# Adding the bias of two feed-forwards on VectorE instead of on TensorE

## The chip, the cores and the metric

The kernel runs on one core of a Trainium2 chip. The metric is the device time of one execution, in microseconds (us); lower is better. A core has TensorE (PE, matrix products into PSUM; PEld is its loading of weights), VectorE (DVE), ScalarE (ACT), GpSimd (POOL) and SyncE (SP), whose queue issues transfers. They run side by side and wait for each other at semaphores.

## The reference

The input is 4096 rows of 256 numbers. Six layers follow each other, each added to its input after a layer norm: a gated feed-forward, a gated delta-rule attention, the feed-forward again, then a binary feed-forward, a state space layer and the binary feed-forward again with the same weights. The change touches the two binary ones:

```
def _L1_ffn_ref(x, weights, scale, bias):
    w = (weights >= 0.0).astype(x.dtype) * 2.0 - 1.0
    y = jnp.einsum('bsi,oi->bso', x, w)
    y = y * scale + bias
    y = jnp.clip(y, -MAX_VAL, MAX_VAL)      # 100
    return y
...
x = x + 0.5 * _L1_ffn_ref(_layernorm(x), weights, scale, bias)
```

## The kernel before, in words

The program has seven phases, one after the other; each engine has its own sequence of instructions, and between two phases all engines wait for each other (L172). The phases of interest are the last three: `binary` pass 0 (from 988 us), `space` (the state space layer, from 1051 us) and `binary` pass 1 (from about 1186 us, its products from 1197 us).

The rows are held as 32 tiles of 128 rows. A *block* is four tiles (8 blocks), a *pair* is two tiles (16 pairs, P0 to P15, two per block). For a pass:

- ScalarE normalizes the rows of a block (L518) with factors that GpSimd works out from VectorE's statistics. In pass 1, VectorE makes the statistics (L312, L313) of block b+3 just before it takes out the pairs of block b, GpSimd makes its factors (L304 to L307; L306 is a power) just before it adds the pairs of block b, and ScalarE normalizes block b+3 when it has copied the turned block b+1.
- TensorE turns a block (L625, eight records) and ScalarE copies it from PSUM (L670). TensorE's order is: products of block b, turning of block b+2.
- For each pair, TensorE fills one bank of PSUM (128 x 512): first a product that writes the bias into both halves (L636: a 64x128 matrix of 1/32 with a 64x256 matrix of the bias, its first 32 rows being the rounded half bias and the next 32 what the rounding left), then four products with `w_bin` on top (L641, eight records in the trace). Pair p uses bank p mod 4 and waits until pair p-4 has been taken out.
- VectorE takes the pair out of PSUM with a clip to -50 and 50 (L710) into `Y`; GpSimd adds `Y` to the rows (L747).

The factor 0.5 is folded into weights and bias beforehand: at the start of pass 0, VectorE multiplies `w_bin` by half the scale (L700), halves the bias row (L701) and makes the two parts for the product (L696, L702, L703); TensorE's first product waits for `b_weights`, raised by the last of these.

Pass 0 has more in it, for the layer behind it. SP moves each finished block into another order of rows (L764, eight transfers per block). VectorE makes statistics of the moved block b-2 after the pairs of block b, GpSimd its factors (L555 to L558, block b-3), ScalarE its rows from b = 4 on. From block 5 on TensorE also flips two stretches of rows (L576), VectorE multiplies them by gamma (L581, before the pairs) and GpSimd adds beta (L587, after the pairs). In pass 1 SP sends each finished block out (L769).

`own.seq` makes an engine wait for its own instruction before the next one. `bcast_mid(row, 2)` reads a row of 256 twice, for the two halves of a bank.

Of the kernel before, what the change touches and what calls it, by code (L numbers as in the profile page):

```python
# [6 lines left out]
F32R = mybir.dt.float32r  # L7
I32 = mybir.dt.int32
ALU = mybir.AluOpType
# [3 lines left out]
P = 128  # L13
DM = 256
KD = DM // P
# [38 lines left out]
def bcast_mid(ap, n):  # L54
    return ap.unsqueeze(1).to_broadcast([ap.shape[0], n, ap.shape[1]])
# [14 lines left out]
def build(nc, io):  # L70
    ctx = ExitStack()
    with ctx:
# [6 lines left out]
        B = Box()  # L79
# [41 lines left out]
        S = Box()  # L121
# [12 lines left out]
        made = {}  # L134

        def phase_memory(kind, shape, within=None):

            mem = ExitStack()

            def take(name, cols):  # L140
                return mem.enter_context(nc.sbuf_tensor(f"{kind}_{name}", [P, cols], F32))[:]

            M = Box()
            if within is not None:
                within(M)
            shape(M, take)
            made[kind] = M
            return mem

        phase_memory("ffn", ffn_memory).close()  # L150
        both = phase_memory("both", shared_memory)
# [7 lines left out]
        phase_memory("delta", delta_memory, of_both).close()  # L159
        both.close()  # L160
        late = phase_memory("late", late_memory)
        B.X2, B.MV2, B.rows = made["late"].X2, made["late"].MV2, made["late"].rows
        B.rstd2, B.shift2, B.U, B.N2 = made["late"].rstd2, made["late"].shift2, made["late"].U, made["late"].N2
        B.bias_parts, B.thirty_second = made["late"].bias_parts, made["late"].thirty_second
        phase_memory("binary", binary_memory).close()
        phase_memory("space", space_memory).close()
        late.close()
# [142 lines left out]
def tile_stats(v, own, B, X, MV, t):  # L310
    s = B.stats[:, 6 * (t % BLK):6 * (t % BLK) + 6]
    own.seq(v.bn_stats(s, X[:, t, :]))  # L312
    return v.bn_aggr(MV[:, t, :], s)  # L313
# [229 lines left out]
def moved_stats(v, own, B, S, b):  # L543

    v.wait_ge(S.late_in[b], 64 + 128)
    for t in (2 * b, 2 * b + 1, TB + 2 * b, TB + 2 * b + 1):
        i = tile_stats(v, own, B, B.X2, B.MV2, t)
    i.then_inc(S.m_stats, 1)
# [22 lines left out]
def input_flip(pe, B, S, k):  # L571

    pe.wait_ge(S.n_xn, k + 1)
    if k >= 2:
        pe.wait_ge(S.n_gamma, k - 1)
    pe.matmul(B.bank[6 + k % 2][:], B.flip, B.N2[k % 2], start=True, stop=True).then_inc(S.n_flip, 1)  # L576


def input_strength(v, B, S, k):
    v.wait_ge(S.n_flip, k + 1)  # L580
    v.tensor_tensor(both_of(B.U, k), two(B.bank[6 + k % 2][:]), bcast_mid(B.rows[2], 2), ALU.mult).then_inc(S.n_gamma, 1)  # L581
# [17 lines left out]
def late_memory(M, take):  # L599

    M.X2 = take("X", NT * DM).rearrange("p (t d) -> p t d", t=NT)
    M.MV2 = take("mean_var", 2 * NT).rearrange("p (t two) -> p t two", two=2)
    M.rstd2, M.shift2 = take("rstd", NT), take("shift", NT)
    M.U = take("U", NT * DM).rearrange("p (t d) -> p t d", t=NT)
    M.N2 = [take(f"N2{i}", 2 * DM) for i in range(2)]
    M.rows = [take(f"{n}_row", DM) for n in ("scale", "bias", "gamma", "beta")]
    M.bias_parts, M.thirty_second = take("bias_parts", DM), take("thirty_second", P)


def binary_memory(M, take):  # L610
# [5 lines left out]
def binary_tensor(pe, B, M, S, run):  # L616
    blocks, pairs = run * NBLK, run * NT // 2

    def turn(b):
        pe.wait_ge(S.b_xn, blocks + b + 1)  # L620
        for k in range(KD):
            if blocks + b > 0:
                pe.wait_ge(S.b_xt, 2 * (blocks + b - 1) + k + 1)
            for j in range(BLK):
                i = pe.transpose(B.bank[4 + k][:, j * P:(j + 1) * P], M.xn[b % 2][:, j * DM + k * P:j * DM + (k + 1) * P], B.ident)  # L625
            i.then_inc(S.b_xt_ps, 1)

    def project(b):
        pe.wait_ge(S.b_xt, 2 * (blocks + b) + 2)
        pe.wait_ge(S.b_weights, 1)  # L630
        for h in range(2):
            p = 2 * b + h
            if p >= 4:
                pe.wait_ge(S.b_clip, pairs + p - 3)
            o = B.bank[p % 4]
            pe.matmul(o.rearrange("p (j n) -> p j n", j=2), B.thirty_second[0:64, :].bitcast(F32R),  # L636
                      B.bias_parts[0:64, :].bitcast(F32R).unsqueeze(1).to_broadcast([64, 2, DM]),
                      start=True, stop=False, skip_group_check=True)
            for j in range(2):
                for k in range(KD):  # L640
                    i = pe.matmul(o[:, j * DM:(j + 1) * DM], M.XT[b % 3][k][:, (2 * h + j) * P:(2 * h + j + 1) * P],  # L641
                                  B.w_bin[:, k * DM:(k + 1) * DM], start=False, stop=(k == KD - 1), skip_group_check=True)
            i.then_inc(S.b_mm, 1)

    turn(0)
    turn(1)
    for b in range(NBLK):
        if run == 0 and b >= FLIP_LAG:
            input_flip(pe, B, S, 2 * (b - FLIP_LAG))
            input_flip(pe, B, S, 2 * (b - FLIP_LAG) + 1)  # L650
        project(b)
        if b + 2 < NBLK:
            turn(b + 2)
# [30 lines left out]
def binary_vector(v, own, B, M, S, run):  # L684
    pairs = run * NT // 2

    def stats(b):
        for t in range(BLK * b, BLK * b + BLK):
            i = tile_stats(v, own, B, B.X2, B.MV2, t)
        i.then_inc(S.b_stats, 1)  # L690

    def weights():

        scale_row, bias_row = B.rows[0], B.rows[1]
        parts = B.bias_parts.bitcast(F32R)
        v.tensor_scalar(B.thirty_second[0:64, :].bitcast(F32R), B.ident[0:64, :], 0.0, 1.0 / 32, ALU.mult, ALU.add)  # L696
        v.wait_ge(S.rows_in, 64)
        for k in range(KD):
            w = B.w_bin[:, k * DM:(k + 1) * DM]
            v.scalar_tensor_tensor(out=w, in0=w, scalar=0.5, in1=scale_row, op0=ALU.mult, op1=ALU.mult)  # L700
        own.seq(v.tensor_scalar(bias_row, bias_row, 0.5, None, ALU.mult))  # L701
        own.seq(v.tensor_copy(parts[0:64, :], bias_row[0:64, :]))  # L702
        v.tensor_tensor(parts[32:64, :], bias_row[32:64, :], B.bias_parts[32:64, :], ALU.subtract).then_inc(S.b_weights, 1)  # L703

    def clip(b):
        for p in (2 * b, 2 * b + 1):
            v.wait_ge(S.b_mm, pairs + p + 1)
            if p >= 4:
                v.wait_ge(S.b_x, pairs + p - 3)
            v.tensor_scalar(M.Y[p % 4], B.bank[p % 4], -50.0, 50.0, ALU.max, ALU.min).then_inc(S.b_clip, 1)  # L710

    if run == 0:
        weights()
    else:
        for b in range(3):
            stats(b)
    for b in range(NBLK):
        if run == 1 and b + 3 < NBLK:
            stats(b + 3)
        if run == 0 and b >= FLIP_LAG:  # L720
            input_strength(v, B, S, 2 * (b - FLIP_LAG))
            input_strength(v, B, S, 2 * (b - FLIP_LAG) + 1)
        clip(b)
        if run == 0 and b >= STATS_LAG:
            moved_stats(v, own, B, S, b - STATS_LAG)
# [1460 lines left out]
```

## Time and profile before

| | |
|---|---|
| Three timed runs | 1249.26, 1244.98, 1247.41 us; median 1247.41 |
| Profiled execution | 1248.46 us; its span, first to last instruction, 1246.7 us |
| Mean granted TensorE clock | 0.92 |
| Busy: PE, PEld | 1041.7 us (84%), 743.2 us (60%) |
| Busy: DVE, ACT, POOL | 935.5 us (75%), 601.0 us (48%), 520.3 us (42%) |
| L641, the products of the pairs | 256 records, 66.8 us busy |
| L710, the clip from PSUM | 32 instructions, 22.1 us busy |

A time in the trace is counted from the start of the span. An instruction's row gives its start, its duration, its engine and line, what it writes and reads, and in brackets how long its engine had been idle and who released it. TensorE's records overlap and their ends are modelled, so that the distance between two starts says more than a duration. The granted clock is 1.0 at TensorE's upper level and 0.5 at its lower; a mean between the two is a window in which it changed.

### The profile page before, as it was taken

Reading aid. Unit: us, or ns where it says so; the run is one execution under the profiler, and the core shown is the slowest. Engines: PE = TensorE matmul, PEld = TensorE weight load, DVE = VectorE, ACT = ScalarE, POOL = GpSimd, SP = SyncE. Lnnn points to the kernel's source line nnn. Section 1 sums busy time; section 2 is a strip of 40 time slices with the busy share of each in tenths; the row PEclk is TensorE's granted clock in tenths of the full one; section 3 lists DMA queues with packets and bytes.
Section 4 is the critical chain, followed back from the end, with each engine's and each line's share of the span. In section 5 each row is a group of like instructions: output and inputs, shape, how many; then the busy total and the mean of one; then the engine's idle time right before and its main releaser. Section 6 shows DMA issues by size and latency. Waiting matters only on the chain. (4 is left out here: it accounts for less than half of the span.)

```text
span 1246.7 us, 38552 instructions
## 1 busy us (share of the span) xinstructions
PE 1041.7 (84%) x15542; PEld 743.2 (60%) x15542; DVE 935.5 (75%) x2403; ACT 601.0 (48%) x1614; POOL 520.3 (42%) x772
## 2 busy tenths in 40 slices
PE   2999977777888888888898876579999798799878
PEld 2888853444555555555565655458888674355456
DVE  3777736378899999999999988527776445899853
ACT  2433345435666767677766664554333343101052
POOL 2666530423444334444344443216666257400055
PEclk9999988887899999999999987769999798899979
DMA  9000013344344434344434432100000023954013
GB/s 249 20 2 1 1 56 110 79 97 105 82 97 103 96 91 102 80 106 103 97 91 92 100 90 70 37 3 1 1 1 1 18 66 95 244 153 118 1 34 101
DMA packets 220160, 93.30 MB, mean 75 GB/s; under 512 B 143440, under 2 KB 209872, under 8 KB 219984
## 3 DMA queue, kind: packets, MB, share of 16 engines
q1 hardware_dynamic: 212240, 79.83, 26.1%
q0 software_dynamic: 6144, 8.40, 2.8%
q10 hardware_dynamic: 1600, 2.62, 0.7%
q8 instruction: 123, 2.02, 0.7%
q14 instruction: 53, 0.43, 0.1%
HBM read 56.20 MB, written 30.41 MB: 69 GB/s over the span
## 5 line engine op out<-in xcount | busy, mean ns | idle before, releaser
L1762 DVE TENSOR_TENSOR delta_tmp<-delta_PR 128x130 f32<-128x130 f32 (+12 forms) x416 | 162.3, 390 | 9.4
L1759 DVE TENSOR_TENSOR delta_PR<-delta_PR,delta_tmp 128x130 f32<-128x130 f32 (+12 forms) x416 | 157.7, 379 | 9.4
L1886 POOL TENSOR_TENSOR delta_S<-delta_E,delta_Bm 128x128 f32<-128x128 f32 x32 | 15.2, 476 | 226.7 <-issue 220.1
L1414 PE MATMUL psum<-delta_T,delta_pad 128*32 128x128 f32 x2048 | 82.3, 328 | 30.7 <-DMA delta_T<-inverse_scratch 29.8
L1613 ACT ACTIVATE delta_y<-psum 32x128 f32<-32x128 f32 x256 | 68.7, 268 | 59.8 <-PE psum L1448 56.9
L1414 PEld LDWEIGHTS psum<-delta_T,delta_pad 128*32 128x32 f32 x2048 | 70.2, 134 | 41.5 <-DMA delta_T<-inverse_scratch 34.8
L507 POOL TENSOR_TENSOR ffn_H<-ffn_hid,ffn_H 128x512 fp32r<-128x512 f32 x48 | 61.6, 1289 | 59.2 <-DVE ffn_H L473 59.2
L507 POOL TENSOR_TENSOR first_H<-first_hid,first_H 128x512 fp32r<-128x512 f32 x48 | 61.6, 1289 | 53.0 <-DVE first_H L473 53.0
L1629 ACT ACTIVATE delta_wide<-delta_S 32x128 f32<-32x128 f32 x256 | 78.2, 305 | 3.2
L1398 PE MATMUL psum<-delta_MV,delta_KT 32*32 32x128 f32 x2048 | 69.6, 289 | 10.7 <-ACT delta_E L1563 10.7
L1873 POOL DMA_DIRECT2D delta_Kd<-key_scratch x128 | 74.7, 590 | 0.1
L1398 PEld LDWEIGHTS psum<-delta_MV,delta_KT 32*32 32x32 f32 x2048 | 59.4, 113 | 22.4 <-ACT delta_E L1563 15.5
L1358 PE MATMUL psum<-both_w_in,delta_xT 128*128 128x512 f32 x128 | 66.7, 645 | 3.3 <-DVEq L172 2.1
L439 ACT ACTIVATE first_silu<-psum 128x512 f32<-128x512 f32 x48 | 28.8, 599 | 83.3 <-PE psum L392 83.3
L439 ACT ACTIVATE ffn_silu<-psum 128x512 f32<-128x512 f32 x48 | 28.8, 599 | 81.1 <-PE psum L392 81.1
L312 DVE BATCH_NORM_STATS2 ln_stats<-X 128x6 f32<-128x256 f32 x128 | 54.1, 423 | 17.4 <-DMA X<-in_x 14.8
L641 PE MATMUL psum<-w_bin,binary_XT 128*128 128x256 f32 x256 | 66.8, 406 | 0.0
L1368 PE MATMUL psum<-both_w_in,delta_xT 128*128 128x512 f32 x128 | 64.4, 627 | 0.0
L710 DVE TENSOR_SCALAR binary_Y<-psum 128x512 f32<-128x512 f32 x32 | 22.1, 692 | 54.0 <-PE psum L641 53.9
L1850 POOL TENSOR_TENSOR delta_VK<-delta_QK,both_eg 128x256 f32<-128x256 f32 x32 | 21.1, 660 | 88.7 <-DVE delta_QK L1694 88.5
L1461 PEld LDWEIGHTS psum<-delta_y,delta_Kd 32*32 32x32 f32 x2048 | 23.1, 111 | 57.5 <-ACT delta_y L1613 57.5
L392 PE MATMUL psum<-first_XT,w_gate 128*128 128x512 f32 x192 | 54.0, 404 | 3.7 <-DVE first_XT L461 3.7
(284 smaller groups left out, 2685.6 us busy)
## 6 DMA issues: line engine op xcount, KB each, us to landing
within_scratch<-delta_PT SPq DMA_DIRECT2D x128, 64.0 KB, 1.9
delta_PR<-within_scratch SPq DMA_DIRECT2D x16, 512.0 KB, 4.4
inverse_scratch<-delta_PR SPq DMA_DIRECT2D x16, 512.0 KB, 3.0
space_T<-taps_scratch SPq DMA_DIRECT2D x8, 1024.0 KB, 5.9
X<-taps_scratch SPq DMA_DIRECT2D x8, 1024.0 KB, 8.8
X<-in_x SPq DMA_DIRECT2D x32, 128.0 KB, 9.9
turned_scratch<-gates_XT SPq DMA_DIRECT2D x16, 256.0 KB, 2.3
delta_xT<-turned_scratch SPq DMA_DIRECT2D x32, 128.0 KB, 3.0
```

Source lines behind the costliest of these rows:

```text
L439: a.activation(M.silu[n % 3], B.bank[n % 2][:], ACT.Silu, scale=1.0 / 127.0).then_inc(S.silu, 1)
L507: g.tensor_tensor(lo.bitcast(F32R), M.hid[n % 3], hi, ALU.subtract).then_inc(S.hid_lo, 1)
L641: i = pe.matmul(o[:, j * DM:(j + 1) * DM], M.XT[b % 3][k][:, (2 * h + j) * P:(2 * h + j + 1) * P], B.w_bin[:, k * DM:(k + 1) * DM], start= ...
L1358: i = pe.matmul(bank[4][:], M.xT[t % 2][:, k * P:(k + 1) * P], M.w_in[:, k, 0:512], start=(k == 0), stop=(k == 1))
L1368: i = pe.matmul(bank[5][:], M.xT[t % 2][:, k * P:(k + 1) * P], M.w_in[:, k, 512:1024], start=(k == 0), stop=(k == 1))
L1398: mm = pe.matmul(kk[g][rows, q * P:(q + 1) * P], M.KT[rows, g * P + SUB * q:g * P + SUB * q + SUB], M.MV[rows, (4 * g + q) * P:(4 * g + q ...
L1414: i = pe.matmul(bank[3][SUB * c:SUB * c + SUB, (2 * w + g) * P:(2 * w + g + 1) * P], M.pad[:, from_c:from_c + SUB], M.T[t % 2][:, h * P:(h ...
L1613: i = a.activation(dst, heads(bank[6][rows, half * P:(half + 1) * P]), ACT.Copy)
L1629: i = a.activation(states(M.wide[half])[rows, :, SUB * c:SUB * c + SUB], states(X)[rows, :, :], ACT.Copy)
L1759: i = v.tensor_tensor(after, after, t3, ALU.add)
L1762: i = v.tensor_tensor(t3, column.to_broadcast([P, j, n_after]), row.to_broadcast([P, j, n_after]), ALU.mult)
L1873: g.dma_start(dst, src).then_inc(S.k_in[t % 2], 16)
```

## The change

The product of the bias goes, and with it its two matrices. A pair's four products start the bank themselves. VectorE adds the halved bias row as it takes the pair out of PSUM, into `Y`, waits for that, and clips `Y` in place in SBUF. `b_weights` is raised by the second product of weights and scale; the halving of the bias row stands behind it.

```diff
 def late_memory(M, take):
-    M.bias_parts, M.thirty_second = take("bias_parts", DM), take("thirty_second", P)
...
 def project(b):
...
             o = B.bank[p % 4]
-            pe.matmul(o.rearrange("p (j n) -> p j n", j=2), B.thirty_second[0:64, :].bitcast(F32R),
-                      B.bias_parts[0:64, :].bitcast(F32R).unsqueeze(1).to_broadcast([64, 2, DM]),
-                      start=True, stop=False, skip_group_check=True)
             for j in range(2):
                 for k in range(KD):
                     i = pe.matmul(o[:, j * DM:(j + 1) * DM], M.XT[b % 3][k][:, (2 * h + j) * P:(2 * h + j + 1) * P],
-                                  B.w_bin[:, k * DM:(k + 1) * DM], start=False, stop=(k == KD - 1), skip_group_check=True)
+                                  B.w_bin[:, k * DM:(k + 1) * DM], start=(k == 0), stop=(k == KD - 1))
             i.then_inc(S.b_mm, 1)
...
 def weights():
         scale_row, bias_row = B.rows[0], B.rows[1]
-        parts = B.bias_parts.bitcast(F32R)
-        v.tensor_scalar(B.thirty_second[0:64, :].bitcast(F32R), B.ident[0:64, :], 0.0, 1.0 / 32, ALU.mult, ALU.add)
         v.wait_ge(S.rows_in, 64)
         for k in range(KD):
             w = B.w_bin[:, k * DM:(k + 1) * DM]
-            v.scalar_tensor_tensor(out=w, in0=w, scalar=0.5, in1=scale_row, op0=ALU.mult, op1=ALU.mult)
+            i = v.scalar_tensor_tensor(out=w, in0=w, scalar=0.5, in1=scale_row, op0=ALU.mult, op1=ALU.mult)
+        i.then_inc(S.b_weights, 1)
         own.seq(v.tensor_scalar(bias_row, bias_row, 0.5, None, ALU.mult))
-        own.seq(v.tensor_copy(parts[0:64, :], bias_row[0:64, :]))
-        v.tensor_tensor(parts[32:64, :], bias_row[32:64, :], B.bias_parts[32:64, :], ALU.subtract).then_inc(S.b_weights, 1)
...
 def clip(b):
         for p in (2 * b, 2 * b + 1):
             v.wait_ge(S.b_mm, pairs + p + 1)
             if p >= 4:
                 v.wait_ge(S.b_x, pairs + p - 3)
-            v.tensor_scalar(M.Y[p % 4], B.bank[p % 4], -50.0, 50.0, ALU.max, ALU.min).then_inc(S.b_clip, 1)
+            y = M.Y[p % 4]
+            both = B.bank[p % 4].rearrange("p (j n) -> p j n", j=2)
+            own.seq(v.tensor_tensor(y.rearrange("p (j n) -> p j n", j=2), both, bcast_mid(B.rows[1], 2), ALU.add))
+            v.tensor_scalar(y, y, -50.0, 50.0, ALU.max, ALU.min).then_inc(S.b_clip, 1)
```

## Rows read from the trace of the kernel before

**Rows 1.** The chain that ended last, in order of time: start us, us, what.
```profile
1197.14 0.72 PE psum L636
...
1200.65 0.43 PE psum L636
1201.08 1.92 PE psum L641 x8
1203.00 0.87 PE psum L625 x8
```

**Rows 2.** Window of pass 1: busy us of PE, PEld, DVE, ACT, POOL; clock; DMA.
```profile
1197.00:1242.20 45.20, 44.19 (x193) 32.29 (x192) 19.05 (x48) 17.75 (x36) 25.85 (x32) 0.97 0.24 82
```

**Rows 3.** Single lines of VectorE: duration ns min/median/max, first and last start.
```profile
L710 DVE TENSOR_SCALAR binary_Y<-psum x32: 691/692/693, 1000.1 to 1241.2; 128x512 f32<-128x512 f32 x32
...
L581 DVE TENSOR_TENSOR late_U<-psum,late_gamma_row x16: 656/682/692, 1028.2 to 1090.6; 128x512 f32<-128x512 f32 x16
...
L478 DVE TENSOR_SCALAR first_raw_bin<-first_raw_bin x1: 421/421/421, 130.4 to 130.4; 128x512 f32<-128x512 f32 x1
```

**Rows 4.** Timeline around the start of pass 0: start us, us, engine.
```profile
994.44 0.28 DVE L701 TENSOR_SCALAR late_bias_row<-late_bias_row 128x256 f32<-128x256 f32 x1
994.76 0.28 DVE L702 CAST late_bias_parts<-late_bias_row 64x256 fp32r<-64x256 f32 x1
995.08 0.41 DVE L703 TENSOR_TENSOR late_bias_parts<-late_bias_row,late_bias_parts 32x256 fp32r<-32x256 f32 x1
...
995.64 0.76 PE L636 MATMUL psum<-late_bias_parts,late_thirty_second 64*128 64x512 f32 x1 [3.18 <-DVE late_bias_parts L703]
...
996.33 3.78 PE L641 MATMUL psum<-w_bin,binary_XT 128*128 128x256 f32 x8
...
1000.76 2.38 PE L641 MATMUL psum<-w_bin,binary_XT 128*128 128x256 f32 x8
```

**Rows 5.** Windows of 1 us, columns as in rows 2: the clock is 0.70 and 0.72.
```profile
1001.00:1002.00 1.00, 1.00 (x4) 0.86 (x5) 0.00 (x0) 0.00 (x0) 1.00 (x1) 0.70 0.00 0
...
1199.00:1200.00 1.00, 1.00 (x5) 0.84 (x4) 0.00 (x0) 1.00 (x3) 0.00 (x0) 0.72 0.00 0
```

**Rows 6.** Timeline of GpSimd in pass 0, from block 5.
```profile
1028.41 0.24 POOL L555 TENSOR_SCALAR late_shift<-late_mean_var 128x4 f32<-128x4 f32 x1 [0.88 <-DVE late_mean_var L313]
...
1037.38 0.24 POOL L555 TENSOR_SCALAR late_shift<-late_mean_var 128x4 f32<-128x4 f32 x1
...
1040.85 1.27 POOL L747 TENSOR_TENSOR X<-binary_Y,X 128x512 f32<-128x512 f32 x1 [0.32 <-DVE binary_Y L710]
...
1044.67 0.24 POOL L555 TENSOR_SCALAR late_shift<-late_mean_var 128x4 f32<-128x4 f32 x1
...
1049.00 2.48 POOL L587 TENSOR_TENSOR late_U<-late_U,late_beta_row 128x512 f32<-128x512 f32 x2
```

**Rows 7.** Timeline of one block in pass 1: statistics, factors, rows.
```profile
1203.65 0.42 DVE L312 BATCH_NORM_STATS2 ln_stats<-late_X 128x6 f32<-128x256 f32 x1
...
1205.95 0.24 POOL L304 TENSOR_SCALAR ln_shift<-late_mean_var 128x4 f32<-128x4 f32 x1 [0.87 <-DVE late_mean_var L313]
...
1207.91 2.08 ACT L518 ACTIVATE binary_xn<-late_X,ln_shift,ln_rstd 128x256 f32<-128x256 f32 x4 [3.35 <-POOL ln_shift L307]
```

**Rows 8.** Timelines where a CAST of VectorE meets GpSimd.
```profile
945.05 1.29 POOL L507 TENSOR_TENSOR ffn_H<-ffn_hid,ffn_H 128x512 fp32r<-128x512 f32 x1
945.10 1.52 DVE L473 CAST ffn_H<-ffn_hid 128x512 fp32r<-128x512 f32 x1
...
131.41 1.04 POOL L306 TENSOR_TENSOR ln_rstd<-ln_rstd,minus_half 128x4 f32<-128x4 f32 x1
131.88 0.43 DVE L473 CAST first_H<-first_hid 128x512 fp32r<-128x512 f32 x1
```

**Rows 9.** Timeline of SP's queue: the last block moved in pass 0.
```profile
1049.07 5.06 SPq L764 DMA_DIRECT2D late_X<-X  x8
```

**Rows 10.** Timeline of GpSimd: the last addition of pass 1.
```profile
1242.00 1.26 POOL L747 TENSOR_TENSOR late_X<-binary_Y,late_X 128x512 f32<-128x512 f32 x1 [1.09 <-DVE binary_Y L710]
```

More of the change, by code:

```diff
@@ L163, in build @@
         B.rstd2, B.shift2, B.U, B.N2 = made["late"].rstd2, made["late"].shift2, made["late"].U, made["late"].N2
-        B.bias_parts, B.thirty_second = made["late"].bias_parts, made["late"].thirty_second
         phase_memory("binary", binary_memory).close()
```

## The prediction

> **What bounds the kernel now.** I read the page's chain first, then the stages around the change, then single instructions. The binary feed-forward is computed twice: pass 0 begins near 988 us, pass 1 near 1197 us; I call their 16 bank-sized products P0 to P15. The chain in order of time [rows 1] shows pass 1 as TensorE from end to end: a bias product (0.43 us, the first 0.72 at the lower clock), four 128x256 products in 1.92, and after every second pair the turning of a block, 0.87. The stage table agrees: TensorE is busy for 44 of 45 us, VectorE for 19, GpSimd for 26 [rows 2]. What ends pass 0 is GpSimd instead: its last two offset additions run to 1051.48, and from its factors at 1037.38 on it has no idle except 0.32 us [rows 6].
>
> **The change part by part.** *The weights.* TensorE now waits for the second weight product instead of for L703. Those three bias instructions stand between 994.44 and 995.49; TensorE started at 995.64, 0.15 after [rows 4]. It will start near 994.6, 1.0 earlier. The constant of 1/32 that goes was made under the wait for the rows: nothing.
>
> *The bias products.* 32 go, 0.43 us each at the upper clock and 0.72 at the lower [rows 1]. All sit on TensorE's own sequence.
>
> *The addition.* VectorE's one instruction from PSUM (0.69) becomes an addition from PSUM and a row, then a clip in SBUF. The first is the shape of L581 (PSUM and a row repeated, 128x512): 0.68. The second is the shape of L478 (SBUF to SBUF, 128x512): 0.42 [rows 3]. The wait on its own semaphore between them is about 0.03, the gap between L701 and L702 (994.76 after 994.44 + 0.28 [rows 4]). So 1.14 in place of 0.69: +0.45 per pair, 14.4 us more VectorE work in 32 pairs. The bank is released 0.45 later too, but a product waits for the release of the fourth before it, over 7 us back: no cost.
>
> Is VectorE then the bound? In pass 1 its block is four statistics (from 1203.65 to just before GpSimd takes them up at 1205.95: 2.2) and two pairs (2.3): 4.5 us. TensorE's block goes from 5.57 to 2 x 1.92 + 0.87 = 4.71. GpSimd's is its factors (1205.95 to 1207.88, when ScalarE takes them up: 1.93) and two additions of 1.26: 4.5 [rows 7, 10]. All three fit, with 0.2 us to spare. TensorE stays the bound if nobody holds VectorE up.
>
> *The lock.* Something does. At 945.10 a CAST of 128x512 in SBUF, alone 0.43, lasts 1.52 beside a GpSimd addition that had begun 0.05 before: it ended 0.28 after it. But at 131.88 a CAST of that shape runs in its full 0.43 inside GpSimd's small power operation [rows 8]. I take it that the new clip is held for up to 1.1 by GpSimd's 128x512 additions, and not by its small factors; the addition from PSUM isn't held. The Trainium skill, page "SBUF — State Buffer", section "Who interferes with whom", states this lock for a whole instruction, with any GpSimd instruction; the first row agrees with it and the second doesn't.
>
> *Pass 1, walked.* The clock rises at 1199.56 (mean 0.72 over 1199 to 1200 [rows 5]), whoever is running. Four products are eight records: 3.78 / 8 = 0.47 us each at the lower clock [rows 4], 1.92 / 8 = 0.24 at the upper [rows 1]. P0 now starts them at 1197.14: 2.42 us at the lower clock are 5.1 records, the other 2.9 take 0.69, and it ends at 1200.25, 0.4 earlier than 1200.65. Then 15 x 1.92 and six turnings of 0.87 put P15 at 1234.3, where by the same count (15 x 2.35) it was 1241.1; GpSimd's last addition began at 1242.00, 0.09 + 0.69 behind 1241.2 [rows 10]. VectorE: pairs P0 and P1 are clipped by 1203.35, statistics of block 4 end at 1205.5, its factors at 1207.5; P2 is clipped at 1206.6, but its addition must wait for the factors and takes GpSimd at 1207.5, just as the clip of P3 wants it at 1207.6: held to 1209.0. Statistics of block 5 end at 1211.2. Walked on in the same way, blocks 6 and 7 follow at 1215.7 and 1220.2, with no hold or one more. Block 7's factors are there at 1222.6 and its rows (four, 2.07) at 1224.7; its turning comes at 1225.7. No turning waits, by a margin of 1 us. The tail grows by the +0.45 behind P15. Gain: 6.9 - 0.45 = 6.4 us.
>
> *Pass 0, walked.* The 1.0 from the weights; P0 and P1 mostly run before the clock rises (at about 1001.7; if that moves with the start, at 1000.6), so P1 ends at 1001.3 to 1001.9 in place of 1003.14 [rows 4, 5]: I take 1.55. Eight pairs of 0.43 more make 5.0 at the end of P9: 1020.5, where 1003.14 + 8 x 2.35 + 4 x 0.87 was 1025.4. A part is given back by the lag of VectorE and GpSimd: the clip of P7 meets the addition of P6 and is held to 1017.8, statistics of block 1 end at 1020.0, their factors at 1022.0, only then come the additions of P8 and P9, to 1024.9. So GpSimd's block 5 begins near 1024.95, 3.45 earlier than 1028.41. From there GpSimd is the bound: its block is 7.29 (1037.38 to 1044.67) less 0.32 = 6.97, the last 6.81, so 20.75 in three blocks, where they took 23.07 [rows 6]: 2.3 more. VectorE's clips hold it up in turn (0.42 at most, some two times): -0.7. TensorE (flips 1.7, pairs 3.84, turning 0.87: 6.4) and VectorE (two strengths 1.25, pairs 2.3, statistics 2.2, holds 1 to 1.5: 7.0) are below or beside it. Transfers of a moved block take SP 5.06 [rows 9] and pass 0's early blocks now come every 4.7, so SP lags, but by my walk each block lands 1 to 4 us before its statistics. Gain: 3.45 + 2.3 - 0.7 = 5.0 us, with bounds 2.5 (each of six clips holds GpSimd up and is held) and 6.8 (no lock).
>
> *The stage between* starts cold on TensorE in both kernels, after 5 us of idleness now and 8 then, so it moves as a whole: nothing.
>
> **Sum.** 5.0 + 6.4 = 11.4 us. The profiled execution took 1248.46 (span 1246.7 and 1.8 around it), 1.05 above the median of the three timed runs; against the median, 1247.41 - 11.4 = 1236.0. 0.3% (3.7 us) is about what a measurement of this kernel can tell from no change.
>
> **The rivals.**
> 1. *The lock makes VectorE the pace of pass 1.* If GpSimd's power operation (1.04) holds the clip as well, the first clip of a block waits 0.9 and the second 0.9 to 1.1: VectorE's block becomes 6.0, for the four blocks with statistics. Block 7's statistics end at 1223.5, its turning at 1228.5, P15 at 1236.2: 1.9 lost; pass 0 loses about as much. Total gain 7 to 8: 1239.5. The row at 131.88 speaks against, the margin of 0.2 us per block for. 25%. It is the result that the skill's rule for whole instructions (the same page and section) would give.
> 2. *Pass 0 gives nothing.* GpSimd, VectorE and SP together keep the old pace there, and only pass 1 and the start gain: 6.4 to 7.5, so 1240.5. For: GpSimd ends the pass, and no work leaves it [rows 6]. Against: it has 2.3 us to catch up from block 5 on, and before that it followed TensorE's pace of 5.57 with a block of 4.5. 10%.
> 3. *The gain vanishes in new waits,* less than 3.7 us left: every clip held for 1.09 (VectorE's block 6.7) and every addition of GpSimd held for 0.42: P15 near 1242 and pass 0 gains 2.5. 1245. 6%.
> 4. *Slower: TensorE loses its clock.* It stands at the lower level after the 3.2 us of idleness before 995.64, for some 6 us [rows 4, 5]. If statistics, factors and rows of a block (2.2 + 1.9 + 2.1) came late enough to idle TensorE by 3 us before each of four turnings, each would cost 3 and some 2.5 to 3 at half speed: 4 x 5.8 = 23 against 11.4, so 1259. It decides from the second such gap on (2 x 5.8 = 11.6). My margin at the turnings is 1 us, and a lag of VectorE of 0.2 to 1 us per block doesn't make gaps of 3. 5%.
> The forecast itself, gains of 9 to 12.8: 54%, its own range 1234.5 to 1238.5.
>
> **How the numbers follow.** The likeliest case gives 1236.0. The range reaches down to no lock and a full 6.8 in pass 0 (13.3: 1234) and up past rivals 1 and 2 to 1242; 85% of the chance lies in it. Faster by over 0.3%: the forecast, rivals 1 and 2 = 0.89. Within 0.3%: 0.06. Slower: 0.05.
>
> **What would show it.** In the profile after: no L636; pass 1's chain on TensorE as 1.92, 1.92, 0.87 with no gap above 0.2; the new addition at 0.68 and the clip at 0.42 when free, 1.0 to 1.5 in about one of four; GpSimd without idle from block 5 of pass 0 and its end near 1046.5; pass 1's P15 35 to 38 us after the start of P0, against 44.0. Wrong would be: clips held inside the power operation, turnings waiting for ACT's rows, a phase end of pass 0 later than 1049, or a clock below 1.0 after the first 4 us of either pass.

## The result, and the profile after

The kernel after takes 1231.16 us (median of five timed runs, 1228.71 to 1234.12), the kernel before 1247.41 (1244.98 to 1250.18): a ratio of 0.9864, with a 95% interval of 0.9846 to 0.9881. It is 16.3 us faster. The forecast was 11.4 us faster, 1236.0, with a range down to 1234 (13.3 us of gain): the sign and the mechanism came out, the size was five microseconds short.

The profiled execution after took 1231.16 us (span 1229.0), 17.3 less than the one before. I cut both traces at the same events: the first turning of pass 0, the first product of the stage between, the first pair product (or bias product) of pass 1, and the end of GpSimd's last addition.

| us | before | after | change | forecast |
|---|---|---|---|---|
| pass 0 (988.57 to 1051.59 before, 988.75 to 1045.32 after) | 63.02 | 56.57 | -6.45 | -5.0 |
| the stage between | 145.48 | 143.89 | -1.6 | 0 |
| pass 1 | 46.18 | 36.34 | -9.8 | -6.4 |

The stage between is the same code in both kernels. Over the executions of this study it lies between 142.67 and 145.48, and the kernel after alone shows 143.89 and 142.67 in two of them. I don't count its 1.6 us as the change's. The phases ahead of pass 0, also the same code, end anywhere from 984.4 to 993.0 us, which is why I compare passes and medians and not spans. So the miss is in the passes: 1.45 us in pass 0, 3.4 in pass 1, together 4.9, where the median is off by 4.8.

The chain that ended last, of the kernel after, in order of time (start, us, what), answers to [rows 1]:

```profile
1189.42 3.55 PE psum L636 x16
1192.97 0.87 PE psum L623 x8
1193.84 3.46 PE psum L636 x16
...
1202.50 3.46 PE psum L636 x16
1205.95 1.01 PE psum L623 x8
1206.96 3.46 PE psum L636 x16
1210.42 0.10 issue
1210.52 1.07 PE psum L623 x8
1211.58 3.46 PE psum L636 x16
...
1215.04 1.06 PE psum L623 x8
1216.11 5.20 PE psum L636 x24
...
1221.33 0.70 DVE binary_Y L704
...
1222.05 0.44 DVE binary_Y L705
1222.49 0.07 issue
1222.56 1.26 POOL late_X L742
```

In the kernel after, L636 is the pair's products, L623 the turning, L704 the new addition and L705 the clip in SBUF. TensorE is still the pace. But two pairs, 16 records, take 3.46 us, 1.73 each. In [rows 1] the same four products of a pair, eight records, took 1.92. A pair lost not only its 0.43 but 0.19 more: that is the number this study is about. The turnings are 0.87 at first and 1.01 to 1.07 for blocks 5, 6 and 7. (The chain turns off at P14; P15 passes VectorE from 1223.05 on, and GpSimd's last addition ends at 1225.55.)

The window of pass 1 after, columns as in [rows 2], and the two instructions of VectorE (duration in ns as min/median/max, first and last start), which answer to [rows 3]:

```profile
1189.42:1225.57 36.15, 33.49 (x176) 28.78 (x175) 26.57 (x64) 17.60 (x35) 27.39 (x32) 1.00 0.31 102
```

```profile
L704 DVE TENSOR_TENSOR binary_Y<-psum,late_bias_row x32: 657/691/695, 998.8 to 1223.1; 128x512 f32<-128x512 f32 x32
L705 DVE TENSOR_SCALAR binary_Y<-binary_Y x32: 426/428/1000, 999.6 to 1223.8; 128x512 f32<-128x512 f32 x32
```

The durations are those forecast, 0.68 and 0.42 against 0.69 and 0.43. VectorE's work in pass 1 went from 19.05 to 26.57 us in a window that is 9 us shorter, and GpSimd's is 27.39 of 36.15.

### The profile page after: what moved, and what is told of

Its sections match the earlier page's. It is cut to its first block and busy times, and to the rows that moved or that the text cites. A ratio compares the mean times of both kernels' runs of the same rounds, so it can differ in the third digit from the quotient of the medians.

```text
span 1229.0 us, 38519 instructions
## 1 busy us (share of the span) xinstructions
PE 1016.6 (83%) x15510; PEld 735.2 (60%) x15510; DVE 949.8 (77%) x2432; ACT 601.3 (49%) x1614; POOL 523.1 (43%) x772
## 5 line engine op out<-in xcount | busy, mean ns | idle before, releaser
L311 DVE BATCH_NORM_STATS2 ln_stats<-X 128x6 f32<-128x256 f32 x128 | 54.1, 423 | 17.3 <-DMA X<-in_x 14.7
L636 PE MATMUL psum<-w_bin,binary_XT 128*128 128x256 f32 x256 | 59.5, 387 | 2.6 <-DVE w_bin L693 2.6
L1282 POOL DMA_DIRECT2D delta_T<-inverse_scratch x64 | 41.6, 657 | 32.5 <-DMA inverse_scratch<-delta_PR 28.0
```

## The experiments

The first question was where 0.19 us per pair came from. The timelines of TensorE's weight loads (PEld) and products in the kernel before, which the chain of waits does not show:

```profile
1206.16 0.18 PEld L636 LDWEIGHTS psum<-late_bias_parts,late_thirty_second 64*128 64x128 f32 x1 [0.33 <-issue]
1206.59 0.94 PEld L641 LDWEIGHTS psum<-w_bin,binary_XT 128*128 128x128 f32 x5 [0.25 <-issue]
```

```profile
1206.16 0.50 PE L636 MATMUL psum<-late_bias_parts,late_thirty_second 64*128 64x512 f32 x1
1206.59 1.78 PE L641 MATMUL psum<-w_bin,binary_XT 128*128 128x256 f32 x7
```

The load of the bias product starts at 1206.16, with its own product and not ahead of it, after 0.33 us without a load; the next one starts with its product too, at 1206.59. The records of the same timeline start at 1205.85 (the last product of the pair before), 1206.16 (bias), 1206.59 and 1206.91 (the first two products of the pair): steps of 0.31, 0.43 and 0.32 us, and then 0.216 from record to record. So of the 0.19 one half lies ahead of the bias product and one half behind it. In the kernel after the loads run on without such a gap:

```profile
1193.90 3.00 PEld L636 LDWEIGHTS psum<-w_bin,binary_XT 128*128 128x128 f32 x14
```

Three properties set the bias product apart from its neighbours: its operands are bitcast to another type (F32R), it multiplies 64 rows and not 128, and it is 512 columns long. The first experiments separate these; the others separate TensorE's share from VectorE's and pass 0 from pass 1. The ratio is that to the kernel before on the same chip, with its 95% interval; the passes are cut as above, in us (in e10 and e11 pass 1 begins with its first two-column product).

| kernel | median | ratio to before | pass 0 | pass 1 |
|---|---|---|---|---|
| e2, both, before + VectorE's addition | 1250.84 | 1.0020 (0.9994 to 1.0047) | 64.07 | 46.62 |
| e3, bias product without the bitcast | 1268.44 | 1.0154 (1.0108 to 1.0199) | 72.57 | 57.23 |
| e4, bias product over 128 rows | 1238.05 | 0.9914 (0.9887 to 0.9941) | 58.26 | 39.33 |
| e5, bias product twice | 1256.94 | 1.0065 (1.0037 to 1.0094) | 66.26 | 48.71 |
| e10, after + 64-row, 2-column product | 1249.62 | 0.9986 (0.9963 to 1.0010) | 62.20 | 45.38 |
| e11, after + 128-row, 2-column product | 1237.74 | 0.9899 (0.9850 to 0.9948) | 57.30 | 40.15 |
| e7, the change in pass 1 alone | 1240.58 | 0.9912 (0.9881 to 0.9942) | 62.95 | 36.35 |
| e9, the kernel after again | 1233.83 | 0.9878 (0.9852 to 0.9905) | 56.78 | 36.80 |
| e1, after without the addition | 1231.49 | 0.9857 (0.9830 to 0.9883) | 54.87 | 35.35 |
| e6, after, sum kept in PSUM | 1234.25 | 0.9873 (0.9848 to 0.9899) | 56.56 | 37.42 |
| e8, after, VectorE adds the last pairs | 1228.65 | 0.9834 (0.9807 to 0.9862) | 54.10 | 36.88 |

**e2_both: VectorE's part alone.** The kernel before with the new addition and clip, and the bias product left where it is.

```diff
-            v.tensor_scalar(M.Y[p % 4], B.bank[p % 4], -50.0, 50.0, ALU.max, ALU.min).then_inc(S.b_clip, 1)
+            own.seq(v.tensor_tensor(y.rearrange("p (j n) -> p j n", j=2), both, bcast_mid(B.rows[1], 2), ALU.add))
+            v.tensor_scalar(y, y, -50.0, 50.0, ALU.max, ALU.min).then_inc(S.b_clip, 1)
```

> The bias product stays on TensorE and VectorE adds the bias as well (the bias counts twice). Theory (the addition on VectorE costs what the prediction said, and the surprise is all on TensorE): TensorE's block stays 5.57 us, the tail grows by 0.45, pass 0 by at most 1; 1247.4 + 0.5 to 1.5 = 1248 to 1249. Rival (VectorE's part is what was misjudged: the change to an addition speeds something up): under 1246.

Pass 0 took 64.07 us and pass 1 46.62, 1.05 and 0.44 more than before; the 0.44 is the longer tail. The ratio can't be told from 1. Its chain keeps the old pair:

```profile
1225.21 0.43 PE psum L636
1225.63 1.92 PE psum L641 x8
```

So the new instructions on VectorE don't shorten the products behind the bias product. Whatever gave the 0.19 back is tied to that product itself.

**e3_plain_f32: the type.** The bitcast is taken off the bias product's operands and off the matrix of 1/32.

```diff
-            pe.matmul(o.rearrange("p (j n) -> p j n", j=2), B.thirty_second[0:64, :].bitcast(F32R),
-                      B.bias_parts[0:64, :].bitcast(F32R).unsqueeze(1).to_broadcast([64, 2, DM]),
+            pe.matmul(o.rearrange("p (j n) -> p j n", j=2), B.thirty_second[0:64, :],
+                      B.bias_parts[0:64, :].unsqueeze(1).to_broadcast([64, 2, DM]),
```

> The bias product in plain f32 in place of f32r, same 64 rows, same bank. Its own columns then cost two records of 512 columns, 0.43 each by the 0.216 of a record of 256: 0.86 per pair. Theory A (the loads of weights lie bare where f32r and f32 products follow each other, 0.41 per pair): nothing is bare any more, a pair is 1.73 + 0.86 = 2.59, a block 6.05, total 1247.4 + 32 x 0.235 = 1255. Rivals B (weights of 64 rows) and C (a product onto the bank just written): the 0.41 stays, a pair is 3.0, a block 6.9, total 1268.

```profile
1235.61 1.05 PE psum L636 x2
1236.66 1.93 PE psum L641 x8
```

The bias product becomes two records in 1.05 us, and the products behind it keep their 1.92, although all of them now have one type. That the change of type costs the 0.19 falls.

**e4_128_rows: the rows.** The product runs over all 128 rows, with a matrix of 1/64; the lower half of the rows holds the rounded bias, the upper half what the rounding left. It computes the same bias.

```diff
-            pe.matmul(o.rearrange("p (j n) -> p j n", j=2), B.thirty_second[0:64, :].bitcast(F32R),
-                      B.bias_parts[0:64, :].bitcast(F32R).unsqueeze(1).to_broadcast([64, 2, DM]),
+            pe.matmul(o.rearrange("p (j n) -> p j n", j=2), B.thirty_second.bitcast(F32R),
+                      B.bias_parts.bitcast(F32R).unsqueeze(1).to_broadcast([P, 2, DM]),
```

> The bias product in f32r over 128 rows (a matrix of 1/64) in place of 64. Theory A (change between f32r and f32) and rival C (the bank just written): nothing changes, block 5.57, 1247.4. Rival B (weights of 64 rows are what is not loaded ahead): the 0.41 goes, a pair is 1.94, a block 4.75, total about 1237.

```profile
1209.36 0.23 PE psum L636
1209.59 1.73 PE psum L641 x8
```

```profile
1198.33 1.05 PEld L641 LDWEIGHTS psum<-w_bin,binary_XT 128*128 128x128 f32 x5
1199.41 0.19 PEld L636 LDWEIGHTS psum<-late_bias_parts,late_thirty_second 128*128 128x128 f32 x1
1199.63 1.71 PEld L641 LDWEIGHTS psum<-w_bin,binary_XT 128*128 128x128 f32 x8
```

Twice the multiplications, and a pair takes 1.96 us in place of 2.35: 0.23 for the bias, 1.73 for the rest. The load of the bias product, at 1199.41, has no idle before it. This kernel, in which VectorE adds nothing, is 10.7 us faster than the kernel before on its chip. Two thirds of what the change brings is to be had by doubling the height of the product that it removes. The product is still 512 columns long and still writes the bank onto which the pair's products then add, so that neither its length nor a product onto a bank just written makes the 0.19.

**e5_twice: the 64 rows, or the step between heights?** Two bias products of 64 rows, one behind the other; the bias is counted twice.

```diff
-            pe.matmul(o.rearrange("p (j n) -> p j n", j=2), ..., start=True, stop=False, skip_group_check=True)
+            for twice in range(2):
+                pe.matmul(o.rearrange("p (j n) -> p j n", j=2), ..., start=(twice == 0), stop=False, skip_group_check=True)
```

> The f32r bias product is made twice in a row (the bias counts twice). Theory A: the second follows one of its own kind, its load is hidden, and it adds its columns only, 0.216 per pair: block 6.0, total 1254. Rivals B and C: it adds 0.43 or more per pair, as 64 rows and the bank just written are there again: block 6.4, total 1261.

```profile
1225.79 0.66 PE psum L637 x2
1226.45 1.92 PE psum L642 x8
```

The second product adds 0.23 us, not 0.43. So 0.23 is what a 512-column product of this type costs at either height, and the remaining 0.39 of a pair is paid once for the way from 128 rows to 64 and back. That a 64-row product is dear as such falls with this run; the step between heights stands.

**e10_short_64 and e11_short_128: the step by itself.** The kernel after with a product of two columns ahead of each pair's products, which the pair then overwrites; the two kernels differ in nothing but its rows.

```diff
+            pe.matmul(o[:, 0:2], B.ident[0:64, :], B.w_bin[0:64, 0:2], start=True, stop=True)
```

```diff
+            pe.matmul(o[:, 0:2], B.ident, B.w_bin[:, 0:2], start=True, stop=True)
```

> The changed kernel, and in front of each pair's products one product of 64 rows with 2 columns in plain f32 (two records), overwritten by what follows. It has next to no columns, so its price is that of the two changes of height. Theory: the loads of weights behind and before a change between 64 and 128 rows aren't made ahead, 0.41 us a pair: with two short records of some 0.06 each a pair is about 2.2 to 2.3 us on TensorE in place of 1.73, pass 1 36.6 to 44 or more. Rival (what costs is the 512 columns onto the bank, or f32r): a pair is 1.73 + 0.1 to 0.2.

> The same with a short product of 128 rows. Theory: no change of height, so only its two short records: a pair is 1.73 + 0.1 to 0.2 us, some 0.3 to 0.4 less than with 64 rows; pass 1 about 38.5. Rival (any product put in front costs an exposed load): the same as with 64 rows.

e10, and below it e11:

```profile
1230.80 0.31 PE psum L634 x2
1231.11 1.92 PE psum L637 x8
```

```profile
1220.61 0.12 PE psum L634 x2
1220.73 1.83 PE psum L637 x8
```

With 64 rows the pair takes 2.23 us, with 128 rows 1.95: 0.28 for the change of height, behind a product that does almost nothing. Times 32 that is 9.0 us; the medians are 11.9 apart, and the passes in the trace 4.9 and 5.2, together 10.1. Part of what goes beyond 9.0 is the clock, which rose later in e10's execution: 6.7 us after the first product of pass 0 (3.5 in e11) and 3.8 after that of pass 1 (1.6 in e11). A product of two columns with 64 rows undoes the whole change (0.9986 of before). A 128-row one isn't free either: 0.22 over the 1.73 of the pair without it.

The Trainium skill, page "TensorE: Matmul & The Clock Gate", section "The mechanism", says that weight loads overlap with running products only when their group of rows differs. The same section also names loads into a background weight buffer, without saying when that is used. These traces show another order than the "only": the 128-row load runs beside 128-row products all the way (spacing 0.216 us, no gap above 0.03 us between loads), and it is the 64-row one among them that starts late. The measurement decides here.

**e7_only_pass1: do the two passes add up?** Pass 0 keeps the bias product and the old clip; pass 1 is as in the kernel after.

```diff
+            if run == 0:
+                pe.matmul(... bias ..., start=True, stop=False, skip_group_check=True)
...
+            if run == 0:
+                v.tensor_scalar(M.Y[p % 4], B.bank[p % 4], -50.0, 50.0, ALU.max, ALU.min).then_inc(S.b_clip, 1)
+                continue
```

> Pass 0 as in the kernel before (bias product of 64 rows, clip from PSUM), pass 1 as in the changed kernel. Theory (the two passes add up): pass 0 63.0 us, pass 1 36.5, total 1247.4 - 9.7 = 1237.5 to 1239. Rival (part of pass 1's gain comes from pass 0 having ended early): above 1241.

Pass 0 is 62.95, as before, and pass 1 36.35, as after: the gain of pass 1 doesn't need that of pass 0. The median is 9.0 us below that of before, against 9.8 in the trace.

**e9_after** is the kernel after once more, beside e1, e6 and e8 on one chip.

> The changed kernel itself again, so that the next three are compared with it on one chip: 1231, pass 1 (from the first product to the end of the last addition) 36.3 us, pass 0 56.6 us.

It comes to the same ratio, 0.9878 against 0.9864, with overlapping intervals.

**e1_no_bias: what VectorE's part costs.** The kernel after with the old clip straight from PSUM; the bias is left out.

```diff
-            own.seq(v.tensor_tensor(y.rearrange("p (j n) -> p j n", j=2), both, bcast_mid(B.rows[1], 2), ALU.add))
-            v.tensor_scalar(y, y, -50.0, 50.0, ALU.max, ALU.min).then_inc(S.b_clip, 1)
+            v.tensor_scalar(M.Y[p % 4], B.bank[p % 4], -50.0, 50.0, ALU.max, ALU.min).then_inc(S.b_clip, 1)
```

> No bias at all: the product is gone and VectorE clips straight from PSUM as before (the bias is left out of the result). What is left against the changed kernel is VectorE's share. Theory: pass 1 loses its tail of 0.45 and the 0.6 by which turnings wait, 36.3 to 35.3; pass 0 loses the lag and the lock, about 1.5; total 1228.5. Rival (VectorE's addition is hidden entirely but for the tail): 1230.5.

```profile
1208.22 0.87 PE psum L623 x8
1209.09 3.46 PE psum L636 x16
1212.55 0.87 PE psum L623 x8
...
1216.88 0.87 PE psum L623 x8
```

Every turning takes 0.87 again: the 1.01 to 1.07 of the kernel after are VectorE's doing. The passes are shorter by 1.7 to 1.9 us (pass 0) and 1.0 to 1.45 (pass 1) than in the two profiled executions of the kernel after, about 3 us in all. By the medians it is 2.3 (1231.49 against 1233.83), with intervals that overlap, and short of the 1228.5 expected; this execution's stage between was 145.39 against 142.67 in e9, so that its profiled time can't settle it. So the passes put the addition at about 3 us at this pace, and the medians don't tell it from nothing. In e2, at the old pace, it cost pass 1 nothing beyond the tail.

**e6_psum: the lock on the clip.** The sum stays in PSUM, and the clip reads PSUM, where GpSimd's work doesn't touch it, but lasts 0.69 in place of 0.43.

```diff
-            own.seq(v.tensor_tensor(y.rearrange("p (j n) -> p j n", j=2), both, bcast_mid(B.rows[1], 2), ALU.add))
-            v.tensor_scalar(y, y, -50.0, 50.0, ALU.max, ALU.min).then_inc(S.b_clip, 1)
+            own.seq(v.tensor_tensor(both, both, bcast_mid(B.rows[1], 2), ALU.add))
+            v.tensor_scalar(M.Y[p % 4], B.bank[p % 4], -50.0, 50.0, ALU.max, ALU.min).then_inc(S.b_clip, 1)
```

> VectorE writes the sum back into PSUM and clips from PSUM into SBUF, so the clip costs 0.69 in place of 0.42 and shares nothing with GpSimd. Theory (the lock costs little; VectorE's own time sets its block): pass 1's block grows from 4.5 to 5.1 in the four blocks with statistics, pass 1 36.3 to 38.5, pass 0 unchanged within 1; total 1233.5. Rival (the lock costs more than 0.3 us a pair): not slower than the changed kernel, 1231 or less.

```profile
L704 DVE TENSOR_SCALAR binary_Y<-psum x32: 691/692/693, 1002.7 to 1227.5; 128x512 f32<-128x512 f32 x32
```

No clip is held (691 to 693 ns, where L705 of the kernel after goes to 1000), and the time is the same, 1234.25 against 1233.83. The 16 clips of pass 1 last 11.1 us here and 8.0 there: being held takes less of VectorE's time than clipping from PSUM. Pass 1 is 0.6 us longer than in e9 (37.42 against 36.80). So this run says that this way round the lock gains nothing; as it also lengthens the clip, it doesn't price the lock by itself.

**e8_last_adds: taking GpSimd's end off pass 0.** As GpSimd ends pass 0, VectorE adds the last two pairs there and the last one of pass 1 itself; GpSimd leaves these out.

```diff
+            if p >= NT // 2 - 2 + run:
+                v.tensor_scalar(y, y, -50.0, 50.0, ALU.max, ALU.min).then_inc(S.b_clip, 1)
+                v.wait_ge(S.b_clip, pairs + p + 1)
+                v.wait_ge(S.b_x, pairs + p)
+                v.tensor_tensor(x, y.rearrange("p (j n) -> p j n", j=2), x, ALU.add).then_inc(S.b_x, 1)
+                continue
```

> The changed kernel with the last additions to the rows made by VectorE instead of GpSimd: pairs P14 and P15 in pass 0, P15 in pass 1. Theory (GpSimd's queue ends pass 0, and the hand-over to it is the tail of pass 1): pass 0 shortens by one to two additions of 1.27, less what GpSimd's offsets hold VectorE up, 56.6 to about 54.5; pass 1 by 0.6 (0.69 in place of 1.27, no hand-over); total 1228. Rival (VectorE or the transfers end pass 0 by now): under 1 us in all, 1230.5.

```profile
1034.36 0.56 POOL L554 TENSOR_SCALAR late_shift<-late_mean_var 128x4 f32<-128x4 f32 x1
...
1036.41 0.27 POOL L557 TENSOR_TENSOR late_shift<-late_shift,late_rstd 128x4 f32<-128x4 f32 x1
1036.63 2.48 POOL L586 TENSOR_TENSOR late_U<-late_U,late_beta_row 128x512 f32<-128x512 f32 x2
```

It has the lowest median of the study: 1228.65, a ratio of 0.9834. Its interval and that of e9 overlap a little (up to 0.9862, from 0.9852), but five of its six times lie below the lowest of e9. Pass 0 falls from 56.8 to 54.1 us: the 2.5 of additions between factors and offsets are gone from GpSimd. Pass 1 is not shorter than in e9 (36.88 against 36.80). Its first 16 records took 4.72 us, the first of them at the lower clock, where e9 had 4.03; this scatter of the first block (3.55 to 4.72 in these profiles) covers a tail that is 0.57 shorter, 1.26 against 0.69 for the last addition.

## Why the prediction fell short, point by point

**The bias products: "32 go, 0.43 us each". This step failed.** The mechanism was right, the term was mis-sized: removing one gives 0.62 (2.35 - 1.73), since the products on either side of it give 0.19 back. I had read 1.92 [rows 1] as the cost of four products, 0.24 a record, and it was their cost beside a product of another height; without it a record takes 0.216. Shown by e4, e5, e10 and e11: the product itself is 0.23, the step between heights 0.28 to 0.39. The hint was in the trace of before, in the idle times of the weight loads. In pass 1 the 14 pairs from the second block on give 8.7 us where I had 6.0. The first block gives 2.3 where I had 0.8: 0.4 of that is the same 0.19, twice, and the rest, 1.1, goes with the clock. I had it rise at 1199.56, "whoever is running"; it rose 2.5 us after the first product before (mean 0.72 over 1199 to 1200 [rows 5]) and 0.3 after (0.76 over 1189 to 1190). This is scatter: in the other executions without a bias product in pass 1 (e1, e6, e7, e8, e9) it rose 0.4 to 2.6 us in. So about 1 us of pass 1's 9.8 is luck of the profiled execution. The turnings take 0.6 back. The last product is 10.3 us earlier, about the sum of these, and the forecast had 6.9. VectorE takes P15 33.8 us after the start of P0, below the 35 to 38 that I had named.

**The addition: right.** 0.69 and 0.43, and a tail 0.45 longer (0.48 between the last product and the last addition's end; 0.44 in e2).

**VectorE's block of 4.5 and GpSimd's of 4.5: right, but the block to hold them against was 4.33 and not 4.71.** TensorE now has 2 x 1.73 + 0.87. The other two are 0.2 slower, where I had counted on 0.2 to spare, and fall behind step by step. ScalarE gets its factors later, so it copies the turned block later, and the next turning needs that bank:

```profile
1207.82 2.07 ACT L517 ACTIVATE binary_xn<-late_X,ln_shift,ln_rstd 128x256 f32<-128x256 f32 x4 [1.58 <-POOL ln_shift L306]
1209.80 1.06 ACT L665 ACTIVATE binary_XT<-psum 128x512 f32<-128x512 f32 x2
```

The copies end at 1210.86, and the turning that begins at 1210.52 lasts 1.07 in place of 0.87. Of the forecast's signs of being wrong one came, if small: a turning that waits for ScalarE. Rival 1 named this wait with its chain; it came without its cause, the power operation, and cost 0.6 us and not 1.9. "No turning waits, by a margin of 1 us" was wrong by this much.

**The lock: where it bites was right, its weight was too high.** A clip that begins well inside a GpSimd addition is held until 0.28 to 0.30 us after the addition's end, and one inside the power operation is not; of each engine the timelines of pass 0:

```profile
1013.13 1.53 POOL L556 TENSOR_TENSOR late_rstd<-late_rstd,minus_half 128x4 f32<-128x4 f32 x1
...
1025.53 1.27 POOL L742 TENSOR_TENSOR X<-binary_Y,X 128x512 f32<-128x512 f32 x1
```

```profile
1014.20 0.43 DVE L705 TENSOR_SCALAR binary_Y<-binary_Y 128x512 f32<-128x512 f32 x1
...
1026.08 1.00 DVE L705 TENSOR_SCALAR binary_Y<-binary_Y 128x512 f32<-128x512 f32 x1
```

The 16 clips of pass 1 last 8.0 us and those of pass 0 8.1, where 16 free ones take 6.8. Seven of the 32 are held, by 0.05 to 0.57 us, 2.4 us in all. I had the number about right (one in four) and the size too high (clips of 1.0 to 1.5 us; the longest took 1.00). e6 shows that keeping the clip in PSUM to avoid this gains nothing.

**The weights: half right.** Pass 0 has its first product 6.47 us after its first turning in place of 7.07 (995.64 [rows 4] less 988.57), 0.6 and not 1.0 earlier. L693, which now releases it, itself waited for the rows' transfer until 994.31.

**Pass 0, walked: right in its order, short in its size.** GpSimd without idle from block 5, as forecast:

```profile
1023.30 0.24 POOL L554 TENSOR_SCALAR late_shift<-late_mean_var 128x4 f32<-128x4 f32 x1 [0.23 <-DVE late_mean_var L312]
...
1027.16 1.27 POOL L742 TENSOR_TENSOR X<-binary_Y,X 128x512 f32<-128x512 f32 x1 [0.36 <-DVE binary_Y L705]
...
1042.72 2.48 POOL L586 TENSOR_TENSOR late_U<-late_U,late_beta_row 128x512 f32<-128x512 f32 x2
```

Its block 5 starts 34.55 us into the pass, where it was 39.84 (988.57 to 1028.41 [rows 6]): 5.3 earlier in place of 3.45. TensorE was further ahead than that by then, for two reasons. The first is the 0.19 per pair. The second is the clock, and here a second step of the forecast failed: I had it rise at about 1001.7, or at 1000.6 if it moved with the start. It rose at 998.3, 3.1 us after the first product, where it had taken 6.0 (0.70 over 1001 to 1002 [rows 5]); the columns are those of [rows 2]:

```profile
997.00:998.00 1.00, 1.00 (x4) 0.76 (x3) 0.00 (x0) 0.00 (x0) 0.00 (x0) 0.50 0.00 0
998.00:999.00 1.00, 1.00 (x6) 0.83 (x5) 0.17 (x1) 0.00 (x0) 0.00 (x0) 0.83 0.00 0
```

So VectorE took P1 2.9 us earlier in the pass than before, where I had 1.55 for its end, and P7 6.6 earlier. By my estimate the clock is 1.4 of this (half of the 2.9 us in which TensorE ran at the upper level and not at the lower: a record takes 0.216 us there and 0.47 at the lower).

Unlike in pass 1 this is not scatter: e1, e6, e8, e9 and e11, which also start without the bias's two parts and have no 64-row product, show 3.2 to 3.5 us, and all kernels with the old start (e2, e3, e4, e5, e7) 5.9 to 6.1. e10, with the new start and 64-row products, shows 6.7. Why it rises sooner is open, and how much of the clock's 1.4 reaches the end of the pass, where GpSimd is the bound, no run separates. It isn't needed for the main finding: e4, whose clock rose as late as before, shortens pass 0 by 4.8.

From GpSimd's block 5 on it takes 21.90 us to the end and took 23.07: 1.2 us against the 1.6 forecast (2.3 - 0.7). Together 6.5. The last pair's products, meanwhile, end 11 us earlier than before: what TensorE gains beyond 6.5 is lost to GpSimd at the end of pass 0, and e8 gets 2.7 of it back.

**The stage between: right**, within its own scatter of some 3 us. This scatter and that of the clock's rise make a single profile unfit for claims of less than 2 us.

**The rivals.** Pass 0 gave 6.45 (against rival 2), the clock did not fall in pass 1 (mean 1.00 from 1189.42 on, against rival 4), and nothing vanished (against rival 3). The case that came is one I had not listed: more than the forecast, because the removed instruction had a cost outside its own row.

Left open: why the loads of a product with another height start late, and why the clock rises sooner in pass 0. For the loads the runs show when it happens and its price, not what in TensorE does it. The reverse case, a 64-row run broken by one 128-row product, was not tried, nor any height but 64.

## What to carry to other kernels

Price an instruction that is to go by the time of the whole repeating unit with and without it, not by its own row: look at its neighbours' spacing (0.216 us, against 0.31 ahead of the odd one here and 0.32 behind the first product that follows it), and at the idle of the weight loads. Before moving a small product to another engine, try giving it its neighbours' height: that was worth 10.7 us here, for a different slice and constant. And when the engine that sets the pace gets faster, compare the others' blocks with the new pace first; a margin of 0.2 us in 4.7 was gone before it was used.

## What the runs showed of the hardware

A product that uses 64 rows among products of 128 rows costs 0.28 us (2 columns, e10 against e11) to 0.39 us (512 columns, before against e4) beyond its own time at the upper clock; two 64-row products in a row pay it once (e5).

A clip of 128x512 in SBUF on VectorE that begins inside one of GpSimd's 128x512 additions, and not at its very end, ends 0.28 to 0.30 us after that addition (seven clips, 0.48 to 1.00 us long in place of 0.43). One that begins in the addition's last 0.06 us is not held, and one inside GpSimd's 128x4 power operation isn't either. The power operation takes 1.04 us, also in the four cases where a clip begins inside it and none was running before. It grows where a clip had begun 0.08 to 0.09 us ahead of it and a second one came inside: 1.53 us at 1013.13, beside clips at 1013.05 and 1014.20, then 1.45 at 1018.89 and 1.23 at 1196.99. For L556, the one of pass 0:

```profile
L556 POOL TENSOR_TENSOR late_rstd<-late_rstd,minus_half x8: 1040/1042/1530, 1013.1 to 1072.6; 128x4 f32<-128x4 f32 x8
```

In e1, where nothing clips in SBUF, its longest is 1042 ns.
